# Masked attention: the key bias as two fp32r contraction rows, the shift on GpSimd, and the last layer's side weights loaded by the sync engine

## What is computed

```python
def _L1_xattn_ref(q, k, v1, mask, W1, b1, W2, b2):
    qp = _proj(q, W1, b1, W2, b2)          # (q W1' + b1) W2' + b2
    kp = _proj(k, W1, b1, W2, b2)
    qk = jnp.einsum('bqd,bkd->bqk', qp, kp) * scale + mask
    return jnp.einsum('bqk,bkd->bqd', jax.nn.softmax(qk, axis=-1), v1)

x = x + _L0_xattn_ref(_layernorm(x), ctx_1024, ...)
x = x + _L0_ffn_ref(_layernorm(x), ...)
x = x + _L1_xattn_ref(_layernorm(x), ctx_1024, ctx_1024, fside_1xSxS2_0, ...)
x = x + _L1_ffn_ref(_layernorm(x), ...)
```

## Time and profile before

| What | us |
|---|---|
| median of 3 runs | 3605.62 (3603.48 to 3608.56) |
| the profiled execution: its time | 3610.11 |
| the profiled execution: its span | 3608.4 |
| masked attention: first DMA issue to last store issue | 2492.78 to 2678.31 |
| first DMA issue of the last layer | 2685.73 |
| PE busy over the span | 3250.0 (90%) |

### The profile page before, as it was taken

The page is one execution under the profiler, slowest core; times in us unless marked ns, Lnnn a source line. Parts: engine busy times, 40 slices in busy tenths (PEclk is TensorE's granted clock), DMA queues, the critical chain, the costliest instruction groups (busy, mean ns, idle before and its releaser), DMA issues. The chain is left out here.

```text
span 3608.4 us, 51546 instructions
## 1 busy us (share of the span) xinstructions
PE 3250.0 (90%) x17336; PEld 2772.8 (77%) x17336; DVE 1960.4 (54%) x3277; ACT 1554.8 (43%) x2947; POOL 841.9 (23%) x1152
## 2 busy tenths in 40 slices
PE   7999979999999987998996886995968999999998
PEld 6989878888888875886885565884756777877776
DVE  3245467777777763555887996553863222222221
ACT  3222266666666652334776775553642111111110
POOL 0000066666666650000000440001730000000000
PEclk9999999999999998999998898997988999999999
DMA  6577654545455425554666676443642100111000
GB/s 182 146 242 229 206 166 145 149 137 150 135 146 152 135 82 198 185 188 150 225 217 218 193 244 214 164 167 112 219 140 79 50 21 21 36 35 36 30 24 12
DMA packets 362213, 503.42 MB, mean 140 GB/s; under 512 B 48835, under 2 KB 227379, under 8 KB 358081
## 3 DMA queue, kind: packets, MB, share of 16 engines
q1 hardware_dynamic: 359130, 491.16, 43.4%
q0 software_dynamic: 2864, 9.42, 0.7%
HBM read 292.83 MB, written 174.08 MB: 129 GB/s over the span
## 5 line engine op out<-in xcount | busy, mean ns | idle before, releaser
L2506 DVE SCALAR_TENSOR_TENSOR lf_hT<-lf_hb,lf_hT 128x512 fp32r<-128x512 f32 x128 | 88.6, 692 | 618.8 <-ACT lf_hT L2571 617.2
L2571 ACT ACTIVATE lf_hT<-lf_hb 128x512 fp32r<-128x512 f32 x128 | 76.6, 599 | 685.2 <-PE lf_py L188 636.3
L769 POOL TENSOR_TENSOR at_prob<-at_prob,at_rec 128x308 f32<-128x308 f32 (+1 forms) x256 | 261.7, 1045 | 264.0 <-DVE at_rec L811 263.4
L904 ACT ACTIVATE at_prob<-at_sc,at_nm 128x77 f32<-128x77 f32 (+1 forms) x1024 | 293.5, 383 | 41.4 <-DVE at_nm L798 41.4
L798 DVE TENSOR_REDUCE at_nm<-at_sc 128x4 f32<-128x308 f32 (+1 forms) x256 | 164.7, 685 | 171.4 <-PE at_sc L958 171.1
L917 ACT ACTIVATE at_pT<-at_tp 128x1024 fp32r<-128x1024 f32 x128 | 131.6, 1028 | 200.8 <-PE at_tp L968 200.8
L186 PE MATMUL lf_hb<-lf_xT,lf_w 128*128 128x512 f32 x512 | 204.9, 400 | 0.0
L188 PE MATMUL lf_hb<-lf_xT,lf_w 128*128 128x512 f32 x512 | 203.7, 398 | 0.0
L187 PE MATMUL lf_hb<-lf_xT,lf_w 128*128 128x512 f32 x512 | 203.2, 397 | 0.0
L188 PE MATMUL lf_py<-lf_w,lf_hT 128*128 128x512 f32 x512 | 202.6, 396 | 0.0
L186 PE MATMUL lf_py<-lf_w,lf_hT 128*128 128x512 f32 x512 | 202.5, 395 | 0.0
(11 more groups left out here) (323 smaller groups left out, 9648.4 us busy)
## 6 DMA issues: line engine op xcount, KB each, us to landing
at_kr<-k_rows SPq DMA_DIRECT2D x256, 128.0 KB, 2.8
at_qs<-at_qst SPq DMA_DIRECT2D x512, 64.0 KB, 2.0
raw_gate<-pg_stage SPq DMA_DIRECT2D x96, 256.0 KB, 2.0
pu_rg<-raw_gate SPq DMA_DIRECT2D x96, 256.0 KB
raw_up<-pu_stage SPq DMA_DIRECT2D x96, 256.0 KB, 2.1
om_raw<-raw_up SPq DMA_DIRECT2D x48, 512.0 KB, 4.1
dn_raw<-raw_up SPq DMA_DIRECT2D x48, 512.0 KB, 3.8
xn_parts<-pr_xturned SPq DMA_DIRECT2D x32, 512.0 KB, 4.9
```

Source lines behind the costliest of these rows:

```text
L769: ins = pool.tensor_tensor(prob[:, i, :, lo:hi], prob[:, i, :, lo:hi], rec[:, z, g, :].unsqueeze(2).broadcast_to([P, 2 * NTE, hi - lo]), A ...
L904: ins = act.activation(prob[:, i, m, lo:hi], sc[n % 2][:, m, lo:hi], ACT.Exp, bias=nm[:, n % 2, g, m:m + 1])
L2506: dve.scalar_tensor_tensor(hT[:, i, 1, :], hb[i][:], 0.0, hT[:, i, 0, :].bitcast(F32), ALU.max, ALU.subtract).then_inc(h_done, 1)
```

## The change

1. **Bias.** The 16 x 256 biases are loaded as `traw` with a sample on each of 16 partitions. ACT makes their fp32r high part, DVE the rest (`tsplit`), SP stores both to a new DRAM tensor `key_biases_split` and loads it back as `trow` with two partitions (high, low). `ones` gets two partitions too, and the bias matmul is now one fp32r matmul with a contraction of two rows. PE waits for `t_ready` ahead of the first scores only; before, it waited for the first load at the top of its stream.
2. **Shift.** DVE's `offset` is gone. DVE writes `minus` = -mean right ahead of `var`, and POOL multiplies it with rstd right behind `deviation`.
3. **Side weights.** The 18 small loads of `LoraSides` are issued by SP (two in each of the slots 3 to 11) and no longer by POOL.
4. **A first power in `down`.** POOL sets a 128x1 tile to one and raises it to the power -0.5 ahead of its loop in `down`.

```diff
@@ down, POOL
+                pool.memset(one[:], 1.0).then_inc(one_made, 1)
+                pool.wait_ge(one_made, 1)
+                pool.tensor_tensor(one[:], one[:], neghalf[:, 0:1], ALU.pow).then_inc(one_raised, 1)
                 with pool.Fori(0, NCH // 2) as it:
@@ masked_attention, tiles
-        trow = ph.sb("trow", [1, B, S])
-        ones = ph.sb("ones", [1, P])
+        traw = ph.sb("traw", [B, S])
+        tsplit = ph.sb("tsplit", [B, 2, S], F32R)
+        trow = ph.sb("trow", [2, B, S], F32R)
+        ones = ph.sb("ones", [2, P], F32R)
@@ SP
-            sp.dma_start(trow[:].rearrange("o b s -> o (b s)"), bias_d.rearrange("c n -> (c n)").rearrange("(o n) -> o n", o=1)).then_inc(m_ready, 16)
+            sp.dma_start(traw[:], bias_d.rearrange("c (b s) -> (c b) s", b=NB)).then_inc(traw_ready, 16)
             load_keys(1)
             load_values(1)
             load_x(2)
+            sp.wait_ge(t_low, 1)
+            sp.dma_start(split_d, tsplit[:].bitcast(F32)).then_inc(t_stored, 16)
             load_keys(2)
             load_x(3)
+            sp.wait_ge(t_stored, 16)
+            sp.dma_start(trow[:].bitcast(F32), split_d.rearrange("b a s -> a b s")).then_inc(t_ready, 16)
             for s in range(LAST + 1):
...
+                for i in (2 * s - 6, 2 * s - 5):
+                    if 0 <= i < sides.LOADS:
+                        sides.load(sp, i)
@@ POOL
                 pool.tensor_tensor(rstd[:, b % 2], var[:], neghalf[:, 0:NK], ALU.pow).then_inc(rstd_ready, 1)
+                pool.wait_ge(rstd_ready, b + 1)
+                pool.tensor_tensor(shift[:, b % 2], minus[:, b % 2], rstd[:, b % 2], ALU.mult).then_inc(shift_ready, 1)
...
-                for i in range(2 * s - 2, 2 * s):
-                    if 0 <= i < sides.LOADS:
-                        sides.load(pool, i)
@@ DVE
+                dve.tensor_scalar(minus[:, b % 2], mv[:, b % 2, :, 0], -1.0, None, ALU.mult)
                 dve.tensor_scalar(var[:], mv[:, b % 2, :, 1], EPS, None, ALU.add).then_inc(var_ready, 1)
-            def offset(b):
-                wait_alone(dve, rstd_ready, b + 1, spacer_d)
-                if b >= 2:
-                    dve.wait_ge(xn_ready, b - 1)
-                dve.scalar_tensor_tensor(shift[:, b % 2], mv[:, b % 2, :, 0], -1.0, rstd[:, b % 2], ALU.mult, ALU.mult).then_inc(shift_ready, 1)
...
-                if 0 <= s + 2 < B:
-                    offset(s + 2)
                 if 0 <= s + 3 < B:
                     statistics(s + 3)
+                if s == FIRST:
+                    dve.wait_ge(t_high, 1)
+                    dve.tensor_tensor(tsplit[:, 1, :], traw[:], tsplit[:, 0, :].bitcast(F32), ALU.subtract).then_inc(t_low, 1)
@@ ACT
                     keys_high(s + 2)
+                if s == FIRST + 1:
+                    act.wait_ge(traw_ready, 16)
+                    act.activation(tsplit[:, 0, :], traw[:], ACT.Copy).then_inc(t_high, 1)
@@ PE
+                    if b == 0 and t == 0:
+                        pe.wait_ge(ones_made, 1)
+                        pe.wait_ge(t_ready, 16)
                     pe.matmul(sc[b % 2][:, t, :], ones[:], trow[:, b, :], start=True, stop=False)
...
-            pe.wait_ge(ones_made, 1)
-            pe.wait_ge(m_ready, 32)
```

More of the change, by code:

```diff
@@ L133, in kernel_program @@
     bias_d = nc.dram_tensor("key_biases", (NCH, CT), F32).ap()
+    split_d = nc.dram_tensor("key_biases_split", (B, 2, S), F32).ap()
     with ExitStack() as top:
@@ L140, in kernel_program @@
         cross_attention(nc, a, x_in, ctx_in, x1, xt_d, wg_d, big, scal, ident, neghalf)
-        quantized_ffn(nc, a, ctx_in, x1, xt_d, wg_d, x2, raw_up, raw_gate, keys_d, bias_d, big, scal, ident)
+        quantized_ffn(nc, a, ctx_in, x1, xt_d, wg_d, x2, raw_up, raw_gate, keys_d, bias_d, big, scal, ident, neghalf)
         with Phase(nc, "lo") as ph:
             sides = LoraSides(nc, ph)
-            masked_attention(nc, a, ctx_in, keys_d, bias_d, x2, x3, sides, ident, neghalf)
+            masked_attention(nc, a, ctx_in, keys_d, bias_d, split_d, x2, x3, sides, ident, neghalf)
             lora_ffn(nc, a, sides, x3, out_f, ident, neghalf)
@@ L1157, in scalar_step, with quantized_ffn @@
             act.activation(self.place(par, half, m, 0), self.turned[m][:], ACT.Copy).then_inc(self.hi_done, 1)
-def quantized_ffn(nc, a, ctx_in, x1, xt_d, wg_d, x2, raw_up, raw_gate, keys_d, bias_d, big, scal, ident):
+def quantized_ffn(nc, a, ctx_in, x1, xt_d, wg_d, x2, raw_up, raw_gate, keys_d, bias_d, big, scal, ident, neghalf):
     xq = nc.dram_tensor("xq", (NCH, P, KD * CT), I16).ap()
@@ L1181, in quantized_ffn @@
             output_maximum(nc, a, ctx_in, keys_d, bias_d, raw_up, gate, sq_d, big, scal, folds, wd, wd_parts, wd_late, ident)
-            down(nc, x1, x2, raw_up, gate, wd, wd_late, scal)
+            down(nc, x1, x2, raw_up, gate, wd, wd_late, scal, neghalf)
 def scale_of(dve, c, scal, big_col, scale, inverse, unit, raw):
@@ L1792, in _, with down @@
                     ins.then_inc(t_full, 1)
-def down(nc, x1, x2, raw_up, gate, wd, wd_late, scal):
+def down(nc, x1, x2, raw_up, gate, wd, wd_late, scal, neghalf):
     NO = 3
@@ L1810, in down @@
         stored, y_free = ph.sem("stored"), ph.sem("y_free")
+        one = ph.sb("one", [P, 1])
+        one_made, one_raised = ph.sem("one_made"), ph.sem("one_raised")
         with nc.Block() as block:
@@ L1912, in _, with masked_attention @@
                                 ins.then_inc(om_used, 1)
-def masked_attention(nc, a, ctx_in, keys_d, bias_d, x2, x3, sides, ident, neghalf):
+def masked_attention(nc, a, ctx_in, keys_d, bias_d, split_d, x2, x3, sides, ident, neghalf):
     NK = S // P
@@ L1930, in masked_attention @@
         rstd = ph.sb("rstd", [P, 2, NK])
+        minus = ph.sb("minus", [P, 2, NK])
         shift = ph.sb("shift", [P, 2, NK])
@@ L1952, in masked_attention @@
         r_ready, c_ready = [ph.sem(f"r_ready{i}") for i in range(NR)], [ph.sem(f"c_ready{i}") for i in range(NC)]
-        m_ready, ones_made = ph.sem("m_ready"), ph.sem("ones_made")
+        m_ready, traw_ready, t_high, t_low, t_stored, t_ready, ones_made = (
+            ph.sem(n) for n in ("m_ready", "traw_ready", "t_high", "t_low", "t_stored", "t_ready", "ones_made"))
         stat_done, mv_ready, var_ready, rstd_ready, shift_ready, xn_ready, spacer_d, spacer_p, spacer_a = (
@@ L2024, in values_low @@
                 pool.tensor_tensor(val[:, b % NB_, 1], cin[:, b % NC], val[:, b % NB_, 0].bitcast(F32), ALU.subtract).then_inc(v_low, 1)
-            pool.memset(ones[:], 1.0).then_inc(ones_made, 1)
+            pool.memset(ones[:].bitcast(F32), 1.0).then_inc(ones_made, 1)
             for s in range(FIRST, B):
@@ L2068, in logits @@
                 dve.wait_ge(s_full, b + 1)
-                dve.wait_ge(m_ready, 32)
+                dve.wait_ge(m_ready, 16)
                 if b >= 2:
@@ L2258, with load @@
     LOADS = 2 * (1 + E) + 2 * 5
-    def load(self, pool, i):
+    def load(self, sp, i):
         layer, i = i % 2, i // 2
@@ L2275, in load @@
         if i == E + 1:
-            pool.wait_ge(self.cleared, 4)
-        pool.dma_start(to, src).then_inc(self.loaded, 16)
+            sp.wait_ge(self.cleared, 4)
+        sp.dma_start(to, src).then_inc(self.loaded, 16)
     def high_parts(self, act):
```

## The result

| What | before | after |
|---|---|---|
| median, us (runs) | 3606.1 (3603.48 to 3608.56) | 3583.31 (3579.38 to 3587.83) |
| the profiled execution: its time, its span | 3610.11, 3608.4 | 3587.83, 3586.1 |
| first DMA issue of masked attention | 2492.78 | 2498.94 |
| from there to the last score group's logits row | 171.5 | 142.1 |
| from that row to the last layer's first load | 21.4 | 21.7 |

A forecast was written before the change was run, and what follows sets the result against it. PE was taken to bound the middle (8.6 us a slot), with an ACT-POOL-DVE loop nearly as long (8.52). Terms 12.1 + 2.7 - 0.1 + 5.9 - 0.3 = 20.3 us took 3605.6 to 3585.3, range 3573 to 3595.

The forecast's parts named there:

- rival 1: Middle: DVE gets in between POOL's two subtractions, logits aren't held, slots of 7.4 us; 30.1 gained, 3575.5; chance 0.18.
- The front: Masked attention up to slot 0: early power, normalization released by the bias's landing, no blocked shift; 12.1 us gained.
- The middle: Ten slots from slot 3: `minus` and `var` stay blocked, loop 8.62 against 8.61 now; -0.1 us.
- the 4.05 us of the earlier trace: Slot 0 before the change: `var` on DVE blocked until the last of four memsets; cited against DVE getting in.
- The loop's length, 8.52: Middle slot: ACT's keys, POOL's two subtractions, DVE's `var`, logits, exponentials; 8.52 us, some 0.08 under PE's slot.
- The bias: PE, between score groups: last product to next group's first falls from 0.83 to 0.24 us; 1.2 saved a sample.
- Slot 0: First slot: DVE can't take its logits before four memsets end, 10.2 us in, hiding PE's late scores; gain 0.
- Slots 1 and 2: The half-clock stretch: cheaper bias groups and earlier transposes, capped at 3.6 by twice the loop; 2.7 us gained.
- The end: From slot 13 to the last scores: PE is the bound again, 20.8 us falls to 14.9; 5.9 gained.
- The border: Behind the stage, up to the next layer's first load: seven more semaphores to clear; -0.3 us.
- Rival 2: Front: the code stall isn't moved, first power stays at 2510; 11.8 us gained, 3593.8; chance 0.06.
- rival 3: Middle: PE's clock falls because PE waits in each slot; at 0.50 a slot is 14.8 us, 3647; chance 0.05.

The follow-up runs named there:

- warm_only: The kernel before plus only the first power on POOL in `down`; ratio 0.9974 to the kernel before, stage 160.6 us against 171.5.
- no_warm: The changed kernel without the first power in `down`; ratio 0.9955 to the kernel before, stage 150.7 us against the changed kernel's 142.1.
- shift_only: The kernel before with only the shift moved (`minus` on DVE, product on POOL); ratio 0.9979 to the kernel before, stage 161.6 us.
- late_minus: The changed kernel with a spare DVE instruction ahead of `minus` in slots 3 to 12; executed once, no ratio; ACT's slots 8.51 to 8.54 us in the first five.
- the probe: The changed kernel with two extra DVE tensor_scalar instructions in slot 0, started during POOL's memsets; executed once, no ratio; the first ended with the third memset.
- bias_only: The kernel before with only the two-row fp32r bias; ratio 0.9989 to the kernel before, stage 163.2 us, mean of slots 3 to 12 8.52.

## Why the prediction was right, and where it wasn't

The sum came out right for the run's median (3585.3, measured 3583.31), but by luck: two large terms were wrong in opposite directions, a third was missing, and the median shows less than the stage gained. In the stage 29.2 us were gained; the forecast's 20.3 and rival 1's 30.1 both lie in the interval of the timed ratio (20 to 31), so the time can't tell them apart. The trace can: rival 1's mechanism is the one at work. Its 30.1 is near by luck too: 5.6 too high in the middle and 1.7 at the end, without slot 0's 4.3 and 1.55 short in slots 1 and 2.

**The front (12.1, measured 12.5)** held step by step: the stall moved and hid, the bias's landing released ACT at 9.4 us instead of 9.6, the blocked shift's 1.6 went (1.8). warm_only and no_warm show it from both sides.

**The middle (-0.1, measured 6.4)** failed at the step "I take it that `minus` and `var` both stay blocked until 2598.25". It rested on one row, the 4.05 us of the earlier trace rows, and that row stood in a chain of memsets; the shift at the very border in question had got out. I set that aside for the kind of instruction. The kind doesn't matter (shift_only); the moment does (late_minus). The moment itself it had right: `minus` 0.35 us ahead of the second subtraction (2595.5 and 2595.85), measured 0.39. The Trainium skill ("SBUF — State Buffer", Who interferes with whom) says that whoever issues first holds the shared port pair for the whole instruction. Read literally, that is what the middle shows, in 0.46 and 2.39 us; in the chain of memsets, the probe's 0.79 us across a border isn't explained by it. The loop's length, 8.52, was right and was measured twice (bias_only, late_minus).

**The bias (0.24 a group, measured 0.52)** failed at "I take one product's 0.12". Around the two-row matmul the trace shows 0.21 ahead and 0.31 behind, where products stand 0.12 apart. The 0.83 of the earlier trace rows held that hint: two gaps of 0.21 and 0.62 around one instruction, which I read as the price of fp32 alone. So a slot gained 0.64 and not 1.2, and rival 1, right in its mechanism, was 5.6 us too high in the middle (12.0 for 6.4).

**Slot 0 (0, measured 4.3)** failed at "DVE can't take slot 0's logits before the four memsets end". The 2.2 us that the prediction itself took off DVE bring `minus` to the border between the two subtractions, ahead of the memsets (4.0 us into the slot, where `var` had come 6.2 into it). A position that is blocked now needn't be one that is blocked after what stands ahead of it has gone.

**Slots 1 and 2 (2.7, measured 4.25)**: the term was sized on a stretch that no longer existed. It counted 2.4 us for two bias groups at half clock; by the 0.31 a group that was measured, doubled for the clock, they are worth about 1.2 (an estimate). And it capped the gain by two slots of the 8.52 loop, which is gone. What was gained is mostly the clock of slot 2, granted 0.65 before, 0.87 in bias_only and 1.00 in shift_only, which gains 4.5 there with the fp32 bias untouched. The held logits made PE idle ahead of it, but bias_only had the same idle and more clock, so the cause of the clock is only in part shown. Either part brings nearly all of the gain, and the sum had no term for the clock.

**The end (5.9, measured 1.9)** is three slots of the bias's 0.63. The term built a pass of 7.4 with PE waiting for the normalization and gave that wait back; since PE never waits in the new middle, there was nothing to give back. It is the same mistake as in the middle, seen from the other side.

**The border (-0.3, measured -0.2)** held. Rival 2 is excluded by the first power at 2505.27 and rival 3 by a clock of 1.00 through the middle.

## What to carry to other kernels

When a short instruction on DVE is blocked by GpSimd, ask at what moment it will arrive after the change, to a few tenths of a microsecond, before asking whether it stays blocked: a start 0.4 or 0.03 us ahead of a border cost nothing here, one 0.02 to 0.04 behind it 2.4 us. Look for pairs that hold each other, such as PE's bias and DVE's shift here (0.9 and 0 alone, 6.4 together), and give no edit its price before the other is set. A matmul with very few contraction rows between full ones should be compared with one padded by zeros: here 0.50 against 0.12 us.
